# Graph attention: wide matmuls for three of four i-tiles, low sums moved out by ScalarE, attention transfers in paced pieces

## The reference

```python
seq = (x @ W_seq).reshape(N, 16, 32)
scores = leaky_relu(seq·a1 [i] + seq·a2 [j], 0.2) + (1 - adj) * -65500
attn = softmax(scores, axis=-1)
hidden = einsum('hij,jhd->ihd', attn, seq).reshape(N, 512)
x = layernorm(x + elu(hidden @ W_out + b_out))
S = (adj + adj.T) / 2 + I;  dinv = rowsum(S) ** -0.5
x = layernorm(x + adj @ (dinv[:, None] * S * dinv[None, :]) @ x)
```

## Time and profile before

| | us |
|---|---|
| median of three runs | 788.06 |
| the profiled execution, its own time | 786.61 |
| span of its profile | 784.8 |
| TensorE busy / VectorE busy / ScalarE busy / GpSimd busy | 749.7 / 554.7 / 409.9 / 130.1 |
| granted TensorE clock, mean of the span | 0.992 |

### The profile page before, as it was taken

How to read it: one execution, slowest core, us unless ns; L and a number is a source line. 1 busy time by engine, 2 the same in 40 slices (tenths; PEclk the granted TensorE clock), 3 DMA queues, 4 the chain that set the end, 5 groups by cost and what they waited for, 6 DMA issues and landing times.

```text
span 784.8 us, 29353 instructions
## 1 busy us (share of the span) xinstructions
PE 749.7 (96%) x13731; PEld 552.4 (70%) x13731; DVE 554.7 (71%) x799; ACT 409.9 (52%) x302; POOL 130.1 (17%) x142
## 2 busy tenths in 40 slices
PE   6999799988999999999999999999999999999997
PEld 2444699988999999999999999444434444444443
DVE  2887899998988999999999983687772211333233
ACT  2874887986977888788897880333321111000000
POOL 0000113012320211101111001364433100000000
PEclk9999799999999999999999999999999999999999
DMA  7992510255313111011110121599119800001111
GB/s 304 413 406 103 235 57 5 84 110 110 56 60 84 58 58 36 26 58 58 58 58 4 58 71 31 97 186 175 54 31 172 119 0 1 18 36 41 41 40 41
DMA packets 17770, 71.65 MB, mean 91 GB/s; under 512 B 2016, under 2 KB 2016, under 8 KB 13408
## 3 DMA queue, kind: packets, MB, share of 16 engines
q1 hardware_dynamic: 13040, 52.99, 17.7%
q0 software_dynamic: 4608, 16.78, 14.1%
HBM read 77.89 MB, written 8.65 MB: 110 GB/s over the span
## 4 chain that ended last, share of the span: by engine, by line
PE 78%; DVE 15%; issue 5%; ACT 1%; DMA 1%; POOL 0%; DVEq 0%; POOLq 0%; SPq 0%; ACTq 0%
PE bank L631 13%; PE bank L534 12%; PE bank L533 12%; PE bank L531 11%; PE bank L618 11%; PE bank L467 7%; PE bank L579 7%; DVE RZ L852 5%; PE bank L587 3%; DVE RG L871 2%; DVE RG L867 2%; DVE RP L816 1%; PE bank L571 1%; DVE MT L892 1%; DMA RZ<-in_L_gnn_W_seq_dram 1%
## 5 line engine op out<-in xcount | busy, mean ns | idle before, releaser
L531 PE MATMUL bank<-RP,RG 128*128 128x66 f16 x4096 | 388.8, 193 | 6.9 <-DVE RG L871 3.6
L534 PE MATMUL bank<-RP,MT 128*128 128x66 f16 x4096 | 388.7, 194 | 3.6 <-issue 3.6
L531 PEld LDWEIGHTS bank<-RP,RG 128*128 128x128 fp8e4 x4096 | 386.3, 98 | 8.3 <-DVE RG L871 3.6
L533 PE MATMUL bank<-RP,RG 128*128 128x66 f16 x4096 | 388.7, 195 | 2.1 <-issue 2.1
L534 PEld LDWEIGHTS bank<-RP,MT 128*128 128x128 fp8e4 x4096 | 386.4, 98 | 3.2 <-issue 3.2
L533 PEld LDWEIGHTS bank<-RP,RG 128*128 128x128 fp8e4 x4096 | 386.4, 97 | 2.7 <-issue 2.7
L689 ACT ACTIVATE RZ<-RZ,TAB 128x2048 int8<-128x2048 f32 x160 | 306.6, 1988 | 15.3 <-DVE RG L867 14.5
L852 DVE TENSOR_SCALAR RZ<-RZ,TAB 128x2048 int8<-128x2048 f32 x96 | 132.3, 1378 | 0.0
L867 DVE TENSOR_TENSOR RG<-RZ,MT 128x512 int32<-128x512 int32 x160 | 121.7, 760 | 0.1
L631 PE MATMUL bank<-RZ,MT 128*128 128x512 f16 x512 | 110.7, 379 | 2.2 <-DVE MT L1023 2.2
L391 POOL TENSOR_TENSOR RP<-SEQ,TAB 128x528 f32<-128x528 f32 x32 | 52.2, 1652 | 331.8 <-DVE RP L818 256.7
(11 more groups left out here) (103 smaller groups left out, 593.2 us busy)
## 6 DMA issues: line engine op xcount, KB each, us to landing
RG<-in_adj_t_dram SPq DMA_DIRECT2D x16, 1024.0 KB, 10.6
RZ<-s_rows_dram SPq DMA_DIRECT2D x16, 1024.0 KB, 5.8
seq_copy_dram<-SEQ SPq DMA_DIRECT2D x1, 4224.0 KB, 14.2
S2Q<-in_adj_p_dram POOLq DMA_DIRECT2D x8, 512.0 KB, 6.3
S2Q<-in_adj_tp_dram POOLq DMA_DIRECT2D x8, 512.0 KB, 11.3
RZ<-in_x_dram SPq DMA_DIRECT2D x16, 256.0 KB, 3.5
RP<-in_adj_p_dram POOLq DMA_DIRECT2D x8, 512.0 KB, 7.1
RP<-in_adj_tp_dram POOLq DMA_DIRECT2D x8, 512.0 KB, 13.8
```

Of the source, the lines that this page charges most:

```text
L531: mm(pb[bank][:, c:c + 2 * DV], step, high, start=(j == 0 and i % IB == 0), stop=(j == NT - 1), skip_group_check=True)
L533: mm(pb[bank][:, c:c + 2 * DV], step, low, start=False, stop=(j == NT - 1), skip_group_check=True)
L534: last = mm(pb[bank][:, c + DV:c + 3 * DV], mask, edge, start=False, stop=(j == NT - 1), skip_group_check=True)
```

## The change

1. *TensorE*: an i-tile has 132 columns of a bank (`WW = 4 * DV`) in place of 99, the last of four still 99. For the three wide ones `both` (blocks 0 to 3, 132 columns) takes the place of high and low; the edge matmul then writes two stretches of 33 columns with 33 between. The fourth i-tile keeps its three matmuls.
2. *Evacuation*: ScalarE copies the low sums into the new tile TB (`low_sums`, two ACTIVATEs from PSUM, 792 and 264 elements, behind its j = 9); VectorE adds the others to them from PSUM (`whole_sums`, 792 and 264 elements, behind step 8), then multiplies by RHO, adds, and clears a part of TB in SBUF (behind step 9).
3. *Operands*: `prep` moves from GpSimd to VectorE, behind step 4, one head ahead.
4. *Transfers*: S1B, W_out, the copy of SEQ and the four panels go in pieces (4, 4, 8 and 4), each released by a count of steps; the panels come one in two heads.
5. *Output stage*: the first two `o_product` run their first 15 j ahead of their last, `take_back` stands ahead of `low_z`, and panels 10 to 15 are loaded and added in turns.

```diff
-    AT_EVAC, AT_HIGH, AT_LOW, AT_HID = 7, 8, 11, 13
+    AT_PREP, AT_EVAC, AT_HIGH, AT_LOW, AT_HID = 4, 7, 8, 11, 13
+    AT_LOWS = 9
...
-            with sp.Fori(1, H // 2) as p:
-                for u in range(2):
-                    h = p * 2 + u
-                    sp.wait_ge(z_ready, h * NV - NV)
-                    sp.wait_ge(g_ready, h * NT - NT)
-                    load_s1(h, u)
+            for q in range(NC):
+                sp.wait_ge(g_ready, q * (NT // NC))
+                ts = slice(q * (NT // NC), (q + 1) * (NT // NC))
+                sp.dma_start(seq_copy.rearrange("p (t h d) -> p t h d", t=NT, h=H)[:, ts, :, :], SEQ[:, ts, :, :]).then_inc(seq_stored, 16)
+            for h in range(2, H):
+                sp.wait_ge(z_ready, (h - 1) * NV)
+                for q in range(NS):
+                    sp.wait_ge(g_ready, (h - 1) * NT + 3 * q)
+                    load_s1(h, q)
...
+            def load_pieces(t, h):
+                for q in range(NS):
+                    blocks = slice(q * (NT // NS), (q + 1) * (NT // NS))
+                    gp.wait_ge(g_ready, h * NT + 3 * q + 1)
+                    gp.dma_start(panel(t)[:, blocks, :], adj_p[t][:, blocks, :]).then_inc(panel_in[t], 16)
...
             for h in range(2, H):
-                prep(h)
-                if 3 <= h < 3 + NQ:
-                    load_panel(h - 3)
-                if 4 <= h < 4 + NQ:
-                    add_panel(h - 4)
-                if 5 <= h < 5 + NQ:
-                    add_diagonal(h - 5)
+                for e in range(NE):
+                    if h == 5 + 2 * e:
+                        load_pieces(e, h - 1)
+                    if h == 6 + 2 * e:
+                        add_pieces(e, h - 1)
+                    if h == 7 + 2 * e:
+                        add_diagonal(e, NS)
...
-                        mm(pb[bank][:, c:c + 2 * DV], step, high, start=(j == 0 and i % IB == 0), stop=(j == NT - 1),
-                           skip_group_check=True)
-                        mm(pb[bank][:, c:c + 2 * DV], step, low, start=False, stop=(j == NT - 1), skip_group_check=True)
-                        last = mm(pb[bank][:, c + DV:c + 3 * DV], mask, edge, start=False, stop=(j == NT - 1), skip_group_check=True)
+                        if i % IB < IB - 1:
+                            mm(bank[:, c:c + WW], step, both, start=(j == 0 and i % IB == 0), **ends)
+                            last = mm(bank[:, c:c + WW].rearrange("p (e c d) -> p e c d", e=2, c=2)[:, :, 1, :], mask,
+                                      PN[:, u, j, 4:6, :], start=False, **ends)
+                        else:
+                            mm(bank[:, c:c + 2 * DV], step, high, start=False, **ends)
+                            mm(bank[:, c:c + 2 * DV], step, low, start=False, **ends)
+                            last = mm(bank[:, c + DV:c + 3 * DV], mask, edge, start=False, **ends)
...
+            def low_sums(h):
+
+                sc.wait_ge(g_used, NG + (h + 1) * NT)
+                if h >= 1:
+                    sc.wait_ge(hid_done, h)
+                A(TB[:, :, 0:IB - 1, :], wide_lows(h % 2), ACT.Copy).then_inc(low_sb, 1)
+                A(TB[:, :, IB - 1, DV:2 * DV], narrow_lows(h % 2), ACT.Copy).then_inc(low_sb, 1)
...
+            def whole_sums(h):
+
+                ve.wait_ge(low_sb, 2 * h + 2)
+                V.tensor_tensor(TB[:, :, 0:IB - 1, :], TB[:, :, 0:IB - 1, :], wide_sums(h % 2), ALU.add).then_inc(banks_free, 1)
+                V.tensor_tensor(TB[:, :, IB - 1, :], TB[:, :, IB - 1, :], narrow_sums(h % 2), ALU.add).then_inc(banks_free, 1)
+
             def scale_sums(h):
 
-                ve.wait_ge(g_used, NG + (h + 1) * NT)
-                own.mark(V.tensor_tensor(rows(T), sums(h % 2, 0), rows(RHO[:, h, :].unsqueeze(2).broadcast_to([P, NT, DV])), ALU.mult))
+                ve.wait_ge(banks_free, 2 * h + 2)
+                own.mark(V.tensor_tensor(TN[:, :, 0, :], TN[:, :, 0, :], RHO[:, h, :].unsqueeze(2).broadcast_to([P, NT, DV]), ALU.mult))
 
             def add_sums(h):
 
                 own.wait(ve)
-                own.mark(V.tensor_tensor(rows(T), sums(h % 2, 1), rows(T), ALU.add))
-
-            def add_low_sums(h):
-
+                own.mark(V.tensor_tensor(ND, TN[:, :, 0, :], ND, ALU.add))
                 own.wait(ve)
-                V.tensor_tensor(rows(ND), sums(h % 2, 2), rows(T), ALU.add).then_inc(banks_free, 1)
+                own.mark(V.memset(TB[:, :, IB - 1, 0:DV], 0.0))
...
             for t in range(NT):
+                take_back(t)
                 low_z(t)
-                take_back(t)
```

More of the change, by code:

```diff
@@ L44, in gat_then_normalised_adjacency @@
     NQ = 4
+    NE = 4
+    NS = 4
+    NC = 8
     NP = 6
@@ L56, in gat_then_normalised_adjacency @@
     GT = 4
-    AT_EVAC, AT_HIGH, AT_LOW, AT_HID = 7, 8, 11, 13
-    assert CW * IB <= 512 and 2 * NB == 8
+    AT_PREP, AT_EVAC, AT_HIGH, AT_LOW, AT_HID = 4, 7, 8, 11, 13
+    AT_LOWS = 9
+    assert WW * (IB - 1) + CW <= 512 and 2 * NB == 8
     ctx = ExitStack()
@@ L384, in _ @@
                                  pattern=[[-1, P]], channel_multiplier=1).then_inc(consts, 1)
[L386 to L396, removed]
             gp.wait_ge(deg_done, 1)
@@ L443, in _ @@
                     x_minus_1(t + 2)
[L444 to L450, removed]
+            for t in range(NQ + NP, NT + 2):
+                if t < NT:
+                    gp.wait_ge(y_ps, t - NQ - NP + 1)
+                    load_panel(t)
+                if NQ + NP < t <= NT:
+                    add_panel(t - 1)
+                if NQ + NP + 1 < t:
+                    add_diagonal(t - 2)
             for t in range(NT):
@@ L584, in y_part @@
                 pe.wait_ge(xl_done, j + 1)
-                for i in range(NQ):
+                for i in range(NE):
                     for l in range(2):
@@ L620, in y_product, with o_product @@
                 last.then_inc(y_ps, 1)
-            def o_product(t):
-                if t < 8:
+            def o_product(t, js):
+                if js[0] == 0 and t < 8:
                     pe.wait_ge(yv_done, t + 9)
-                else:
+                elif js[0] == 0:
                     pe.wait_ge(ov_done, t - 7)
-                for j in range(NT):
+                for j in js:
                     if t == 0:
@@ L632, in o_product @@
                                   start=(j == 0 and l == 0), stop=(j == NT - 1 and l == 1))
-                last.then_inc(o2_ps, 1)
+                if js[-1] == NT - 1:
+                    last.then_inc(o2_ps, 1)
             pe.wait_ge(v_added, NT)
-            for t in range(NQ, NT):
+            for t in range(NE, NT):
                 y_product(t)
             pe.wait_ge(mt_back, NT)
-            for t in range(NT):
-                o_product(t)
+            for t in range(2):
+                o_product(t, range(NT - 1))
+            for t in range(2):
+                o_product(t, range(NT - 1, NT))
+            for t in range(2, NT):
+                o_product(t, range(NT))
         @block.scalar
@@ L691, in att_head @@
                         high_operands(h + 1)
+                    if j == AT_LOWS and h > 0:
+                        low_sums(h - 1)
             sc.wait_ge(s_sb, NT)
@@ L699, in _ @@
                 att_head(h)
+            low_sums(H - 1)
             def move_hT(t, lo=0, hi=KC, n=None):
@@ L810, in _, with prep @@
             V.memset(RD[:, :], 1.0).then_inc(tabs_done, 1)
+            def prep(h):
+                own.wait(ve)
+                for e, tab in enumerate((EE, FF)):
+                    V.tensor_tensor(V2[:, :, e, :], SEQ[:, :, h, :], tab[:, h, :].unsqueeze(2).broadcast_to([P, NT, DV]),
+                                    ALU.mult).then_inc(v2_ready, 1)
             def low_operands(h):
@@ L892, in fill_empty @@
                 V.tensor_tensor(MT32[:, j, :], MT32[:, j, :], EMP32, ALU.bitwise_or).then_inc(mt_full, 1)
+            own.mark(V.memset(TB[:, :, IB - 1, 0:DV], 0.0))
+            prep(0)
             low_operands(0)
@@ L925, in _ @@
             att_head(H - 1)
+            whole_sums(H - 1)
             scale_sums(H - 1)
             add_sums(H - 1)
-            add_low_sums(H - 1)
             norms(H - 1)
```

78 lines of the change are left out of this document (50 added, 28 removed).

## The result

The changed kernel takes **764.64 us** (median of four runs, 764.39 to 765.85) against 788.08 (four runs): ratio 0.9708, 95% interval 0.9693 to 0.9724, 23.4 us faster. Forecast were 767 and a range of 759 to 777. A second set of five runs gave 764.63. The first matmul of the attention, for one, starts at 88.13 in this one and at 87.00 in one of the second set.

A forecast was written before the change was run, and what follows sets the result against it. TensorE was taken to bound most heads before (24.08 us), VectorE just next, then VectorE at 23.36. Attention -18.9, then +0.2 and -2.1, gave -20.8: median 788.06 to 767, range 759 to 772, to 777 with rivals.

The forecast's parts named there:

- Two matmuls for three: TensorE's attention heads: a wide matmul takes 58.3 ns (bounds 55.0 and 62.7), making a head 23.23 us, 0.85 less.
- The 81 ns for 128 columns: TensorE's wide matmul: a skill-page figure that would put the sum 50 us or more above before; at most 2 in 100.
- VectorE's head: VectorE's work per attention head becomes 23.36 us, plus 2.4 us in all for GpSimd's issues; late next, just over TensorE.
- rival 3: VectorE pays more in the heads: GpSimd's 32 issues (10 us more) or bubbles, 774 to 777 us; 12 in 100.
- The tie: Attention heads: VectorE (23.4 to 23.7) and TensorE (23.2) lie within 0.5 us of each other.
- below 1 ns: Edge matmul's gap in its output: under 1 ns more for each such matmul costs the kernel nothing.
- The stops: TensorE's stops in attention heads, read as late instructions: quarter bursts shrink 11.4 us to about 1; bounds all or none.
- Rival 2: TensorE's stops in the heads stay, since the transferred bytes are the same: 773 us; 10 in 100.
- ScalarE and the waits: ScalarE's head goes from 20.2 to 21.3 us, under 23.4; its new wait and VectorE's in `whole_sums` are covered.
- Start and end: Attention stage's edges: `prep(0)` -0.6, `prep(1)` +1.2 in head 0; behind it +0.2 for `low_sums`, -2.1 for o products.
- Rival 4: Edge matmul in two stretches is slower: at half pace 6.0 us a head, about 852 us; 6 in 100.

The follow-up runs named there:

- experiment 8: Changed kernel without the low matmul of each bank's fourth i-tile (64 fewer matmuls a head): 761.05 us.
- experiment 7: Changed kernel with the wide i-tiles' edge matmul writing 66 columns in one stretch, without the gap (time only): 763.23 us.
- experiment 5: Kernel before with only the paced pieces (S1B, panels, W_out) added: 783.08 us, beside 788.71 for the kernel before in the same set.
- experiment 4: Changed kernel with whole transfers and the panels at the heads of before (the old bursts under wide matmuls): 765.88 us.
- experiment 9: Changed kernel with the o products and `take_back` in the order of before: 767.97 us.
- experiment 3: Changed kernel with whole transfers and each 132-column matmul issued as two of 66 (768 a head): 793.76 us.
- experiment 1: Changed kernel with S1B and the panels in whole transfers again (`NS = 1`): 764.16 us.

## Why the prediction was right

The gain was forecast at 20.8 and measured at 23.4 by the medians, 20.8 by the two profiled executions. That the last two figures agree is luck: to the end of the last matmul of the attention 20.5 us went where 18.9 were forecast, and behind it 0.2 where 1.9 were. By its steps:

- **Two matmuls for three.** 58.3 ns were taken, 57.6 measured, but the edge matmul costs 32.7 and a narrow three 95.3 in place of 31.35 and 94.05, so TensorE's head is 23.43, not 23.23. The Trainium skill (TensorE: Matmul & The Clock Gate, section Wait — 56ns, not 53.3ns?) adds about 2.5 ns to the columns at 2.4 GHz, an estimate of 57.5 for the wide one, and the trace agrees. The 81 ns for 128 columns in a stream of load and matmul pairs, which the Trainium skill has on the same page (section Back-to-back issue gap), do not agree with it. I had given every 66-column matmul one price. By the kernel before's record the three differ too, 29.8 to 32.2 by what they follow.
- **VectorE's head.** 23.36 plus 0.3 for the panels' issues were forecast, 23.22 measured, with 0.1 to 0.2 more in every second of the eight heads with panels (23.34 and 23.41). Every added row was right to 0.1; the issues cost 0.5 us in all, where I had taken 2.4 and rival 3 some 10 more. So the order of the two was wrong by 0.2 us: TensorE bounds and VectorE is next, as experiment 8 shows. The tie was right, the account of who is late was not: with VectorE as the bound the edge matmul's gap, "below 1 ns", was to cost nothing, and it costs 1.4 us (experiment 7).
- **The stops.** This is the step that failed, though the time hid it. The prediction gave the end of the stops to the pieces ("with a quarter of each burst at a time I expect the 11.4 us of stops to shrink to about 1"). They did go, but either half of the change would do most of it: pieces alone 11.4 to 3.9 (experiment 5), wide matmuls with the old bursts 2.4 (experiment 4). Rival 2 ("the stops stay, since the bytes are the same") is wrong for a reason that I did not have: a packet of instructions now lasts TensorE longer, and there are 84 in place of 108.
- **ScalarE and the waits.** Covered, as said: VectorE waits for ScalarE's copies once in the whole span, 8.3 us at the end of head 15, where it has no steps left and TensorE has not ended.
- **Start and end.** `prep(0)` gave 0.7 (0.6 forecast), head 0 lost 1.14 (1.2), the o products gave their 2.1, and in the one traced execution of experiment 9 the clock fell behind the idle time that they take away. Not foreseen: 1.8 us more behind the last output, the price of the pieces.
- **Rival 4**, the slower side: a gap of 33 columns in an output of 66 costs 0.7 ns of some 33, where 10 ns were needed to make the kernel slower. The Trainium skill (PSUM — Partial Sum Buffer, Specifications) says that a non-contiguous pattern slows matmuls significantly. The trace does not agree for this one.

Parts that stand for the 23.4 us: undoing one of them costs 14.9 (the wide matmul), 7.0 (the place of `prep`), 3.3 (the order of the o products), and nothing for the pieces, whose undoing brings back 0.8 us of stops and takes 1.8 off the end. They sum to more than the gain since each covers for another; undoing two (experiment 3) costs 29.

That the stops are late instructions can be read from the packets of the instruction queue, q8, which the traces hold one by one. From before to after, 3072 matmuls and as many loads of stationary operands go and with them 24 packets; in experiment 8, 1024 of each go and with them 8. So a packet holds 256 instructions, 128 pairs of load and matmul. Two stops of before, of 1.70 and 1.51 us in heads 3 and 4, the profile puts down to VectorE and not to "issue", but VectorE's step had then been ready for 8.3 and 8.5 us, so they are of the same kind. The first of them:

```profile
190.94 0.19 PE L531 MATMUL bank<-RP,RG 128*128 128x66 f16 x1 [1.70 <-DVE RG L871]
```

Three things show in the traces:

- *The stops lie on the packets' grid.* Those of before stand at matmul 112 or 113, 619 to 624, and 752 or 753 of their heads, places that are multiples of 128 apart, give or take the few that one head moves against the next.
- *Each follows a packet.* There are 40 stops of 0.15 us or more, in seven kernels, for which VectorE's step lay ready. TensorE starts again 1.23 to 1.56 us after a packet has landed, in every one of them.
- *A late packet stops TensorE only where TensorE uses packets up fast.* With 768 matmuls a head and no other transfers around it, a packet begins 3.2 to 4.6 us behind the one before it (kernel before and experiment 3). In a burst it begins later. A packet lasts TensorE 4.0 us there (128 x 31.35 ns) and 5.2 with 576 matmuls (23.43 / 576 x 128), and of those of experiment 1 one begun 8.3 us behind the one before it still came in time:

| kernel | matmuls a head | packets begun over 6 us behind the one before, heads 1 to 14 | of these with a stop |
|---|---|---|---|
| before | 768 | 7 | 7 |
| experiment 3 | 768 | 9 | 9 |
| experiment 1 | 576 | 9 | 1 |
| experiment 4 | 576 | 7 | 1 |
| changed | 576 | 13 | 0 |

In the 4 us ahead of these late packets of before the DMA engines were 0.6 or more busy with other transfers. Where the burst falls decides too. In heads 6 to 13 of before S1B is issued 0.9 to 1.3 us ahead of the start of a packet, which is not late, and nothing stops. In heads 12 and 13 of experiment 3 it is issued 2.5 and 2.2 us after the start of one, the next begins only 4.4 us behind the issue, and TensorE stops for 1.1 and 1.2 us. What holds a packet back within a burst the traces do not say.

## What to carry to other kernels

Where two engines are within a few tenths of a microsecond a round, sum each one's round from distances of starts and say which is late next; the pace of the round is then known to 1%, though not which of the two sets it. Before pacing transfers, look at how fast TensorE uses up its instructions: many short matmuls stop beside bursts that fewer, longer ones pass with hardly a stop. And look at the end of the program: here the pieces cost 1.8 us there and saved 0.8 of stops in the heads. And work moved to a spare engine is not free if the two hold each other up: two multiplications that took 3.5 us on GpSimd cost VectorE 1.7 there and 1.2 on VectorE itself.

## What was not expected of the hardware

- 768 short matmuls a head with whole transfers lose 18 us to stops, 576 with the same transfers 0.8; TensorE goes on 1.2 to 1.6 us after the packet of instructions that it lacked has landed.
- After 2.16 us of idle time the clock fell to half for some nine matmuls in one execution (0.65 over 4.8 us) and stayed at 1.00 in another kernel's.
- The span ends 4.3 us behind the last output issue where the transfers go in pieces, 2.5 where they go whole, in all fourteen profiled executions.
- A matmul with a gap in its output costs 0.7 ns more.
